# Expert stage of a mixture-of-experts kernel: transposes between the up and the down products, and GpSimd's additions in front of its gathers

## The reference

```
feats   = rfs(xn), weights = rfs(input_weights)      # random features: exp of a projection to 512
attn    = feats @ weights.T                          # 512 x 512
scores  = sigmoid(xn @ router_w)                     # 64 experts in 8 groups
chosen  = 8 best experts of the 4 best groups, weights normalised to 2.5 in sum
per expert: up to 256 of its tokens, in order of token and rank
    h = silu(rows @ gate_w[e]) * (rows @ up_w[e])    # 512 -> 256
    out[token] += weight * (h @ down_w[e])           # 256 -> 512
shared  = silu(xn @ sg) * (xn @ su) @ sd             # for all tokens
```

## Time and profile before

| | us |
|---|---|
| median of 3 runs | 1304.29 (1303.26 to 1367.09) |
| the profiled execution | 1306.46 |
| its span in the profile | 1304.7 |
| PE busy in the span | 1282.5 (98%) |
| DVE, ACT, POOL busy | 913.6, 650.7, 432.7 |
| granted clock of TensorE, mean | 0.995 |

### The profile page before, as it was taken

The page is one execution under the profiler, slowest core; times in us unless marked ns, Lnnn a source line. Parts: engine busy times, 40 slices in busy tenths (PEclk is TensorE's granted clock), DMA queues, the critical chain, the costliest instruction groups (busy, mean ns, idle before and its releaser), DMA issues.

```text
span 1304.7 us, 22618 instructions
## 1 busy us (share of the span) xinstructions
PE 1282.5 (98%) x7591; PEld 1128.0 (86%) x7591; DVE 913.6 (70%) x1786; ACT 650.7 (50%) x1061; POOL 432.7 (33%) x344
## 2 busy tenths in 40 slices
PE   8999999999999999999999999999999999999994
PEld 7888888888888888888889999999999999999994
DVE  7887787867878678785556667666766666676661
ACT  5422233222232222322256787777777777778772
POOL 1000000000000000000014766666767666676753
PEclk9999999999999999999999999999999999999997
DMA  8346554565545655435447999999999999999995
GB/s 290 97 139 154 128 135 109 144 167 127 126 106 142 167 134 124 103 107 135 136 131 242 272 293 288 288 292 286 286 284 290 292 289 292 286 288 293 290 268 65
DMA packets 203800, 263.65 MB, mean 202 GB/s; under 512 B 49268, under 2 KB 138744, under 8 KB 203768
## 3 DMA queue, kind: packets, MB, share of 16 engines
q1 hardware_dynamic: 175096, 191.93, 51.1%
q0 software_dynamic: 28672, 71.32, 23.5%
HBM read 178.18 MB, written 71.39 MB: 191 GB/s over the span
## 4 chain that ended last, share of the span: by engine, by line
PE 98%; DMA 1%; POOL 0%; issue 0%; DVE 0%; ACT 0%; SPq 0%
PE pmm L1265 18%; PE pmm L1263 18%; PE pmm L1264 18%; PE pout L1263 11%; PE pout L1265 11%; PE pout L1264 11%; PE ptr L1498 4%; PE plp L1327 2%; PE plp L1356 1%; PE plp L1336 1%; PE ptr L1275 0%; DMA xbuf<-_L_attn_proj_matrix_dram 0%; DMA out_dram<-outs,slot_cols 0%; POOL out_dram L1624 0%; PE plp L1345 0%
## 5 line engine op out<-in xcount | busy, mean ns | idle before, releaser
L1624 POOL DMA_INDIRECT out_dram<-outs,slot_cols x128 | 226.0, 1766 | 166.4 <-DMA out_dram<-outs,slot_cols 142.7
L1263 PE MATMUL pmm<-xt_hi,proj_hi 128*128 128x256 f32 (+1 forms) x776 | 249.5, 322 | 1.0 <-DVE xt_lo L805 1.0
L1265 PE MATMUL pmm<-xt_hi,proj_lo 128*128 128x256 f32 (+1 forms) x776 | 246.6, 318 | 0.0
L1264 PE MATMUL pmm<-xt_lo,proj_hi 128*128 128x256 f32 (+1 forms) x776 | 246.6, 318 | 0.0
L1263 PE MATMUL pmm<-xt_hi,sgu_hi 128*128 128x256 f32 (+1 forms) x768 | 246.1, 320 | 0.2 <-issue 0.2
L1264 PE MATMUL pmm<-xt_lo,sgu_hi 128*128 128x256 f32 (+1 forms) x768 | 243.4, 317 | 0.0
L1265 PE MATMUL pmm<-xt_hi,sgu_lo 128*128 128x256 f32 (+1 forms) x768 | 243.4, 317 | 0.0
L1608 POOL TENSOR_TENSOR earlier<-earlier,chosen 128x64 bf16<-128x64 bf16 x64 | 24.3, 379 | 614.9 <-DVE chosen L926 611.1
L1614 POOL DMA_INDIRECT xbuf<-rows,slot_cols x128 | 177.3, 1385 | 82.4 <-issue 39.2
L555 ACT ACTIVATE feat<-pmm,ab 128x512 f32<-128x512 f32 x66 | 45.4, 687 | 286.5 <-PE pmm L1265 286.5
L1264 PEld LDWEIGHTS pmm<-xt_lo,proj_hi 128*128 128x128 f32 x776 | 147.8, 190 | 10.2
(11 more groups left out here) (196 smaller groups left out, 2562.6 us busy)
## 6 DMA issues: line engine op xcount, KB each, us to landing
raw<-in_L_ffn_gate_w_dram SPq DMA_DIRECT2D x64, 512.0 KB
raw<-in_L_ffn_up_w_dram SPq DMA_DIRECT2D x64, 512.0 KB
raw<-in_L_ffn_down_w_dram SPq DMA_DIRECT2D x64, 512.0 KB
outs<-in_L_attn_x_dram SPq DMA_DIRECT2D x32, 512.0 KB, 4.0
out_dram<-outs SPq DMA_DIRECT2D x32, 512.0 KB, 3.3
xbuf<-in_L_attn_x_dram SPq DMA_DIRECT2D x52, 256.0 KB, 7.5
raw<-xn SPq DMA_DIRECT2D x52, 256.0 KB, 6.2
rows<-raw SPq DMA_DIRECT2D x39, 256.0 KB, 4.2
```

The costliest lines, as they stand in the source:

```text
L1263: pe.matmul(psum, lh, rh, start=first and n == 0, stop=False)
L1264: pe.matmul(psum, lh, rl, start=False, stop=False)
L1265: ins = pe.matmul(psum, ll, rh, start=False, stop=final and n == len(pairs) - 1)
L1624: pool.indirect_dma_start(out=out, out_offset=bass.IndirectOffsetOnAxis(ap=slot_cols[:, at:at + 1], axis=0), in_=outs[e.b][:, c, :], in_of ...
```

## The change

In the expert stage only.

- TensorE: a stage is now gate and up of e, look-up products, transposes of e + 1, down of e - 1. `e_turn` signals after four transposes and after eight. The first product of an expert's gate reads and writes 64 columns more (320 in place of 256); the products of the gate's second half, which begin with a start of their own, write those columns anew.
- ScalarE: silu of e first, then gate and up weights of e + 1, `xt_hi` of e + 1 in two halves, `hid_hi`, output copies of e - 1, down weights of e, sign sums. The wait for `out_stored` moves into the stage of expert 1, ahead of its output copies.
- VectorE: gate weights lo of e + 1, hid of e, slot weights and `xt_lo` of e + 1 in two halves, up weights lo of e + 1, `hid_lo` of e, down weights lo of e.
- GpSimd: for n from 4 on, additions for n - 4 and then the gather for n.

```diff
--- before.py
+++ after.py
@@ -56,6 +56,7 @@
 CHUNK = 4
 CHUNKS = E // CHUNK
 E_COLS = slice(48, 48 + CAP)
+E_LEAD = 64
 WARM = 26
 
 
@@ -726,8 +727,10 @@
                 act.activation(edn_hi[e.b], raw[e.b][:, GU:], copy).then_inc(edn_hi_made, 1)
 
             def e_turned_hi(e):
-                act.wait_ge(e_turned, e.n + 1)
-                act.activation(xt_hi[e.b][:, :, E_COLS], ptr_e, copy).then_inc(e_xt_hi_made, 1)
+                for half in range(2):
+                    at = slice(2 * half, 2 * half + 2)
+                    act.wait_ge(e_turned, 2 * e.n + half + 1)
+                    act.activation(xt_hi[e.b][:, at, E_COLS], ptr_e[:, at], copy).then_inc(e_xt_hi_made, 1)
 
             def e_silu(e):
                 act.wait_ge(e_gate_done, e.n + 1)
@@ -747,24 +750,25 @@
                     act.activation(outs[e.b][:, c], pout[c], copy, scale=slot_w[e.q][:, c:c + 1]).then_inc(
                         e_out_made, 1)
 
-            def stage(e, next_rows=True, next_weights=True, out_prev=True, look=None):
+            def stage(e, next_rows=True, next_weights=True, out_prev=True, look=None, first=False):
+                e_silu(e)
+                if next_weights:
+                    gate_up_hi(e.next())
                 if next_rows:
                     e_turned_hi(e.next())
-                if next_weights:
-                    gate_up_hi(e.next())
-                e_silu(e)
-                down_hi(e)
                 e_hidden_hi(e)
+                if first:
+                    for b in range(2):
+                        act.wait_ge(out_stored[b], 16 * GROUPS)
                 if out_prev:
                     e_out(e.prev())
+                down_hi(e)
                 if look is not None:
                     sum_signs(look)
 
             e_turned_hi(turn(0))
             stage(turn(0), next_weights=False, out_prev=False)
-            for b in range(2):
-                act.wait_ge(out_stored[b], 16 * GROUPS)
-            stage(turn(1))
+            stage(turn(1), first=True)
             with act.Fori(0, CHUNKS - 2) as m:
                 for k in range(CHUNK):
                     stage(four(2 * m + 1, k), look=m + 2 if k == 1 else None)
@@ -1213,10 +1217,14 @@
                     slot_w_made, 1)
 
             def e_turned_lo(e):
-                dve.wait_ge(e_xt_hi_made, e.n + 1)
+                dve.wait_ge(e_turned, 2 * e.n + 2)
                 slot_weights(e)
-                dve.tensor_tensor(xt_lo[e.b][:, :, E_COLS], ptr_e, xt_hi[e.b][:, :, E_COLS].bitcast(F32),
-                                  ALU.subtract).then_inc(e_xt_lo_made, 1)
+                for half in range(2):
+                    at = slice(2 * half, 2 * half + 2)
+                    dve.wait_ge(e_xt_hi_made, 2 * e.n + half + 1)
+                    dve.tensor_tensor(xt_lo[e.b][:, at, E_COLS], ptr_e[:, at],
+                                      xt_hi[e.b][:, at, E_COLS].bitcast(F32),
+                                      ALU.subtract).then_inc(e_xt_lo_made, 1)
 
             def e_hidden(e):
                 dve.wait_ge(silu_done, e.n + 1)
@@ -1232,19 +1240,22 @@
                                   ALU.subtract).then_inc(e_hid_lo_made, 1)
 
             def stage(e, next_rows=True, next_weights=True, look=None):
+                if next_weights:
+                    gate_up_lo(e.next(), (0,))
+                e_hidden(e)
                 if next_rows:
                     e_turned_lo(e.next())
                 if next_weights:
-                    gate_up_lo(e.next())
-                e_hidden(e)
+                    gate_up_lo(e.next(), (1,))
+                e_hidden_lo(e)
                 down_lo(e)
-                e_hidden_lo(e)
                 if look is not None:
                     look[0](look[1])
 
             e_turned_lo(turn(0))
             output(turn(GROUPS - 1), 3)
-            stage(turn(0), next_weights=False)
+            e_turned_lo(turn(1))
+            stage(turn(0), next_rows=False, next_weights=False)
             stage(turn(1))
             with dve.Fori(0, CHUNKS - 2) as m:
                 for k in range(CHUNK):
@@ -1257,10 +1268,11 @@
 
         @block.tensor
         def _(pe):
-            def products(psum, pairs, first=True, final=True):
+            def products(psum, pairs, first=True, final=True, lead=False):
 
                 for n, (lh, ll, rh, rl) in enumerate(pairs):
-                    pe.matmul(psum, lh, rh, start=first and n == 0, stop=False)
+                    if n > 0 or not lead:
+                        pe.matmul(psum, lh, rh, start=first and n == 0, stop=False)
                     pe.matmul(psum, lh, rl, start=False, stop=False)
                     ins = pe.matmul(psum, ll, rh, start=False, stop=final and n == len(pairs) - 1)
                 return ins
@@ -1492,24 +1504,29 @@
             def e_turn(e):
 
                 pe.wait_ge(gathered[e.b], 16 * CB * (e.i + 1))
-                at_least(pe, e_xt_lo_made, e.n)
+                at_least(pe, e_xt_lo_made, 2 * e.n)
                 for h in range(HB):
                     for c in range(CB):
                         ins = pe.transpose(ptr_e[:, h, c * P:(c + 1) * P], xe[e.b][:, c, h * P:(h + 1) * P],
                                            ident[:])
-                ins.then_inc(e_turned, 1)
+                    if h % 2 == 1:
+                        ins.then_inc(e_turned, 1)
 
             def e_gate_up(e, parts=(0, 1)):
-                pe.wait_ge(e_xt_lo_made, e.n + 1)
+                pe.wait_ge(e_xt_lo_made, 2 * (e.n + 1))
                 at_least(pe, e_hid_made, e.n)
                 for m in parts:
                     pe.wait_ge(egu_lo_made[m], e.n + 1)
                     for i in range(IB):
                         at = [slice(m * HB * I + h * I + i * P, m * HB * I + h * I + (i + 1) * P)
                               for h in range(HB)]
+                        lead = m == 0 and i == 0
+                        if lead:
+                            pe.matmul(pmm[m][:, 0:CAP + E_LEAD], egu_hi[e.b][:, at[0]],
+                                      xt_hi[e.b][:, 0, E_COLS.start:E_COLS.stop + E_LEAD], start=True, stop=False)
                         ins = products(pmm[m][:, i * CAP:(i + 1) * CAP], [
                             (egu_hi[e.b][:, at[h]], egu_lo[e.b][:, at[h]], xt_hi[e.b][:, h, E_COLS],
-                             xt_lo[e.b][:, h, E_COLS]) for h in range(HB)])
+                             xt_lo[e.b][:, h, E_COLS]) for h in range(HB)], lead=lead)
                     ins.then_inc((e_gate_done, e_up_done)[m], 1)
 
             def e_down(e):
@@ -1527,21 +1544,21 @@
             e_gate_up(turn(0), (0,))
             e_turn(turn(1))
             e_gate_up(turn(0), (1,))
+            e_gate_up(turn(1))
             pe.wait_ge(out_free, 2 + J * GROUPS)
             e_turn(turn(2))
-            e_gate_up(turn(1))
             e_down(turn(0))
             with pe.Fori(0, CHUNKS - 2) as m:
                 for k in range(CHUNK):
                     e = four(2 * m + 1, k)
-                    e_turn(e.next())
                     e_gate_up(e)
                     if k == 1:
                         look_up(m + 2)
+                    e_turn(e.next())
                     e_down(e.prev())
             for n in range(E - 6, E - 1):
+                e_gate_up(turn(n))
                 e_turn(turn(n + 1))
-                e_gate_up(turn(n))
                 e_down(turn(n - 1))
             e_gate_up(turn(E - 1))
             e_down(turn(E - 2))
@@ -1630,16 +1647,16 @@
             pool.wait_ge(xn_stored, XN_STD + XN_QUAD * (GROUPS - STD))
             pool.wait_ge(w_stored, 16 * GROUPS)
             for n in range(E):
+                if n == 4:
+                    for b in range(2):
+                        pool.wait_ge(out_stored[b], 16 * GROUPS)
+                if n >= 4:
+                    add_rows(turn(n - 4))
                 if n % CHUNK == 0 and n > 0:
                     pool.wait_ge(slot_cols_made, n // CHUNK + 1)
                 if n >= 2:
                     pool.wait_ge(slot_w_made, n - 1)
                 gather(turn(n))
-                if n == 3:
-                    for b in range(2):
-                        pool.wait_ge(out_stored[b], 16 * GROUPS)
-                if n >= 4:
-                    add_rows(turn(n - 4))
             for n in range(E - 4, E):
                 add_rows(turn(n))
             pool.wait_ge(added, 16 * CB * E)
```

## The result

| | before | after |
|---|---|---|
| median, us | 1304.28 (4 runs, 1303.26 to 1367.09) | 1336.26 (4 runs, 1331.24 to 1338.28) |
| profiled execution; span, us | 1306.46; 1304.7 | 1335.52; 1333.8 |
| PE busy | 1282.5 (98%) | 1284.6 (96%) |

The ratio is 1.0238, 95% interval 1.0222 to 1.0253: slower by 32 us. Some runs, such as that of 1367 us, fall into a second, slower state of the chip and are left out of every ratio. The prediction was 1300 us, range 1290 to 1318, with 0.05 for slower by over 2%; the result lies outside.

What follows compares the result with a forecast made beforehand. It took TensorE and DMA as full in the expert stage, with GpSimd's addition chain ending last. TensorE's -11.7 us was capped by transfers to -5.6, plus 2.0, say -4 with the look-ups' hand-over: 1300 us, range 1290 to 1318.

Steps and rivals of the forecast that it cites:

- Transposes moved: TensorE's transposes put behind the up products: hand-over costs the same, taken as 0, bound 0 to -1.4 us.
- Pitch and the longer product: TensorE's gate and up products: short pitch for most experts, up to -13.4 us; 64 more columns, +1.7 us.
- TensorE's own sum: TensorE alone, shorter pitch plus longer first product: -13.4 + 1.7 = -11.7 us.
- rival 1: TensorE's products keep the long pitch and gathers come late: +3 us, 1307 us; chance 0.28.
- Additions ahead of the gather: GpSimd's order: 0 for the addition chain, gathers 0 to +1.6 us late at the end, gather 4 +2.0.
- ScalarE and VectorE: Rows' halves on both engines have 1.75 us spare; look-up stages cost 0 to +7 us, taken as 0.
- Weights: Gate and up loads have 2.6 us less lead before use: 0 to +14.5 us, taken as 0.
- rival 3: Late up weights stop ScalarE ahead of the rows' halves: +14.5 us, 1319, or +27; chance 0.18.
- The 1% cap of the transfers: DMA transfers let only 1.0% of the addition chain's 557.6 us be gained, -5.6 us.
- Rival 2: Additions follow a faster TensorE, so everything passes: -12 us, 1292 us; chance 0.12.
- Sum: Whole kernel: -5.6 plus 2.0 gives -3.6, say -4 us with the look-ups' hand-over; 1300 us.

Runs made afterwards that it cites:

- gather_first_256: The kernel after with GpSimd's old order (gather n, then additions n-4) and a first gate product of 256 columns; 1320.42 us.
- lead_16: `down_before_rows` with the first gate product 16 columns longer in place of 64; 1305.62 us in one run.
- down_before_rows: `up_behind_rows` with down weights of e ahead of the rows (ScalarE), and down weights and hidden halves ahead of up weights (both engines); 1294.8 us.
- gather_first: The kernel after with GpSimd's order of before (gather n, then additions n-4); 1317.56 us.
- up_behind_rows: `gather_first` with ScalarE taking up weights of e+1 behind the two halves of `xt_hi`; 1307.29 us.
- down_before_rows_additions_first: `down_before_rows` with additions n-4 in front of gather n on GpSimd; 1310.66 us.
- changed_without_down_loads: The kernel after with only 64 of 1024 down weight values per partition loaded from expert 3 on; 1305.1 us.
- lead_on_before: The kernel before with only the first gate product made 64 columns longer; 1305.07 us.
- additions_first_only: The kernel before with only GpSimd's new order (additions n-4, then gather n); 1396.09 us.

## Why the prediction was wrong

- *Transposes moved*: right. From 975.96 to 976.80 the hand-over takes 0.84 us, against 0.88.
- *Pitch and the longer product*: the size is right. TensorE's own sum, -11.7, is near what the best version got: 62 stages x (9.401 - 9.235) = 10.3. That starts that differ by little decide is also what the runs show. Which start gives which pitch was a guess: with down products ahead and no extra columns it is the long one (`gather_first_256` on time, 0 of 42), as rival 1 read it from expert 0, and it is the 64 columns that turn it (`lead_16` against `down_before_rows`).
- *Additions ahead of the gather*: this step failed, and with it the forecast. I gave it 0 to +1.6 us, and 0 for the chain; it costs 19 (1336.3 against 1317.6), 30 or 16 beside the other orders of ScalarE. The lead of one gather was read about right: from the end of its issue to the transposes 8.3 us for expert 63, 8.7 in the mean of experts 8 to 56, and the landing takes 5.4 of them (3.2 to 7.1; I had 3.8 to 5.7). From landing to transposes this leaves 3.3 us in the mean and 0.4 at the least; both can be too long, for the trace of the kernel before lacks some records of landings. One slot later is 9.45 more, the new place of the transposes gives 5.65 back: 3.3 - 9.45 + 5.65 = -0.5, late in the mean, and less than my own bound of 1.6. What I made of it was wrong twice. First, I booked lateness once, "at the end". A wait of TensorE for a gather, which is issued behind an addition, comes back in every stage, and TensorE then runs at the pace of the additions: 33.5 us of waits ahead of the transposes. Second, that pace I took as fixed, "0 for the chain itself"; it went from 9.45 to 9.95.
- *ScalarE and VectorE*, *Weights*: these failed too; taken at 0, bound +14.5 (rival 3, 1319). `gather_first` is that rival: 1317.6, by its mechanism, with 28.5 us of PE's and PEld's rows for `xt_lo`, of which TensorE loses less (above); `up_behind_rows`, which removes the mechanism, gets 10 us back. The error is in what I took: the earlier trace rows show ScalarE waiting for up even before, and the change lets the load land 2.6 us later against its use, more than the 1.75 us of room that I had worked out myself.
- *The 1% cap of the transfers*: too tight. In `down_before_rows` the additions followed TensorE to 9.33 us and DMA to 292 GB/s. Rival 2, everything passes, 1292, describes that kernel best. With the long pitch (`lead_16`) their cycle is 9.45 us, with the short one 9.33: it follows TensorE, and the chain that ends last was not what set the pace.
- *Sum*: along one path of runs, the change is -10.6 us where nothing else waits (1305.4 to 1294.8), +22.8 for its place of the up and down weights (1294.8 to 1317.6), +18.8 for the additions first (1317.6 to 1336.3): +31 us. These are differences between neighbours and add up by themselves; along another path the parts are other ones, as the 16, 19 and 30 us of the additions show. I had the first term in full and let half of it reach the end; the other two stood at 0 and +1.6.

What stays open: why the landing of an addition takes 5.83 us in the kernel after and 5.24 in the kernel before. It isn't GpSimd's order alone: it is 5.63 in `gather_first`, 5.28 in `up_behind_rows` and 5.21 in `down_before_rows`, all with the gather first, and 5.27 in `down_before_rows_additions_first`. The load of the weights is needed for it (`changed_without_down_loads`) and its time in the stage seems to matter (`down_before_rows_additions_first`, where GpSimd's work is the same); which load it is was not tried.

## What to carry to other kernels

Where an engine issues, behind one another, transfers that feed the compute and transfers that drain it and wait for the last landing, a reorder can tie the feed to the drain: read the slack of every feed (landing to use, smallest and mean), and ask whether a wait comes back each round. Of an instruction moved ahead of another on one engine, the wait moves too: put work that waits for a late load behind work that the critical engine needs. And a faster engine shows its gain only when each such wait is gone: the same 64 columns were worth nothing that the intervals could tell in two orders and about 11 us in a third.

## What was unexpected of the hardware

- Most streams of 256-column products keep one of two rhythms, 0.1135 or 0.1178 us each, from start to end, and the start goes with which. Behind 512-column products and on time, an extra of 64 or 128 columns on the first nearly always gives the short one, 16 or none nearly always the long one; behind transposes and on time, 64 columns or none give the long one (61 of 61 experts in `lead_on_before` and in the kernel before, 8 of 11 in `additions_first_only`). A stream that starts late is short in most cases without the columns and in half with them. The cause of the two rhythms stays open.
- The Trainium skill, page "TensorE: Matmul & The Clock Gate", section "Back-to-back issue gap", gives N/2.4 + 2.5, 109 ns for 256 columns, by which the longer product can only cost. It gives this for an isolated product, which my prediction did not say. The runs, where every product follows another, have 113.5 or 117.8 ns and about 11 us between them.
- After an idle of 3.03 us at the end, the down products of `up_behind_rows` go from 0.23 to 0.43 us apart (1287.07 to 1287.50): 512 columns at the lower level of 1.2 GHz; from 1286.2 us on the granted clock is 0.50. The last addition still waited for a landing and not for them. The idle alone does not decide it: in `gather_first` and `changed_without_down_loads`, with the same 3.03 us at the same place, the last products stay 0.23 us apart.
- With the DMA row at 9 in both from slice 23 on, DMA moved 273 GB/s in the kernel after and 292 in the best one, with the same bytes in the same number of packets.
